# Earlier projections of the odd half sequences and another place for GpSimd's bias sums in an attention and expert block

## What is computed

```python
mod = (silu(c) @ wmod).reshape(B, 6, 1, 256)          # sa, ca, ga, sb, cb, gb
h = layernorm(x) * (1 + ca) + sa
qkv = h @ W_qkv.T + b_qkv                              # 16 heads
attn = softmax(Q @ K.T / 4 + causal)
x = x + ga * ((attn @ V) @ W_o.T + b_o)
h = layernorm(x) * (1 + cb) + sb
x = x + gb * experts(h)                                # top 2 of 8, w1 256x512, silu, w2 512x256
```

## Time and profile before

| | us |
|---|---|
| median of 3 runs | 1002.97 |
| lowest, highest | 1001.2, 1007.18 |
| the profiled execution | 1007.08 |
| its span, first to last instruction | 1005.0 |

### The profile page before, as it was taken

The page is one execution under the profiler, slowest core; times in us unless marked ns, Lnnn a source line. Parts: engine busy times, 40 slices in busy tenths (PEclk is TensorE's granted clock), DMA queues, the critical chain, the costliest instruction groups (busy, mean ns, idle before and its releaser), DMA issues.

```text
span 1005.0 us, 19371 instructions
## 1 busy us (share of the span) xinstructions
PE 894.9 (89%) x6100; PEld 532.1 (53%) x6174; DVE 724.2 (72%) x2323; ACT 582.1 (58%) x1271; POOL 355.6 (35%) x311
## 2 busy tenths in 40 slices
PE   5788799998989999889999997879899999999990
PEld 3443335333444443453543452523698899999880
DVE  8788766879756789857688769799637584444488
ACT  3335475766486677676676857657535433343563
POOL 1422021233324113345013444014386465655530
PEclk7899899999999999999999999989999999999996
DMA  8446337236234366250653746205313323222699
GB/s 280 126 65 128 52 64 166 53 50 142 54 48 112 55 118 132 76 77 22 127 95 107 154 73 192 68 25 173 97 52 121 96 70 100 81 74 75 197 295 314
DMA packets 83235, 110.61 MB, mean 110 GB/s; under 512 B 15930, under 2 KB 56434, under 8 KB 83138
## 3 DMA queue, kind: packets, MB, share of 16 engines
q1 hardware_dynamic: 75506, 89.45, 38.7%
q0 software_dynamic: 6816, 18.62, 5.9%
q10 hardware_dynamic: 816, 1.32, 0.4%
HBM read 69.42 MB, written 35.41 MB: 104 GB/s over the span
## 4 chain that ended last, share of the span: by engine, by line
PE 63%; DVE 13%; ACT 10%; issue 6%; POOL 3%; DMA 3%; SPq 1%; another core or an unknown queue 0%; ACTq 0%; POOLq 0%; DVEq 0%
PE PO L1642 10%; PE PY L1519 10%; PE PH L1519 9%; PE PS L1622 8%; PE PM L1599 7%; ACT PR L1008 4%; PE PHT L1727 3%; PE PX L1654 2%; PE PX L1568 2%; DVE MXF L1321 2%; DVE JK L1318 2%; PE PS L1626 2%; ACT SF L991 2%; PE PX L1671 1%; PE PX L1577 1%
## 5 line engine op out<-in xcount | busy, mean ns | idle before, releaser
L1008 ACT ACTIVATE PR<-PS 128x512 f32<-128x512 f32 (+3 forms) x768 | 334.5, 497 | 149.7 <-PE PS L1626 113.0
L1318 DVE CUSTOM_DVE_ANT_0 JK<-PM,MK 128x128 bf16<-128x128 f32 (+3 forms) x512 | 239.5, 484 | 58.0 <-PE PM L1599 56.7
L1599 PE MATMUL PM<-QK 128*128 128x512 bf16 (+3 forms) x725 | 233.9, 330 | 25.5 <-DVE MXF L1321 14.7
L1622 PE MATMUL PS<-QK 128*128 128x512 bf16 (+3 forms) x737 | 236.6, 332 | 17.8 <-ACT PR L1008 12.7
L1321 DVE TENSOR_REDUCE MXF<-PM 128x1 f32<-128x512 f32 x256 | 175.2, 684 | 78.2 <-PE PM L1599 61.4
L1622 PEld LDWEIGHTS PS<-QK 128*128 128x128 bf16 x768 | 75.4, 99 | 177.6 <-ACT PR L1008 111.5
L1642 PE MATMUL PO<-PR,V 128*17 128x512 f32 (+3 forms) x1536 | 163.3, 498 | 0.1
L1599 PEld LDWEIGHTS PM<-QK 128*128 128x128 bf16 x768 | 75.7, 99 | 100.1 <-DVE MXF L1321 35.5
L1519 PE MATMUL PY<-W2S,HT 128*128 x852 | 119.7, 290 | 2.7 <-issue 1.8
L1626 PE MATMUL PS<-MT,identb 128*128 128x128 bf16 x512 | 112.3, 221 | 1.9 <-issue 1.0
L1519 PE MATMUL PH<-W1S,XT 128*128 x426 | 112.6, 400 | 0.8 <-DVE W2S L1473 0.8
(11 more groups left out here) (269 smaller groups left out, 1179.8 us busy)
## 6 DMA issues: line engine op xcount, KB each, us to landing
QK<-SD SPq DMA_DIRECT2D x180, 128.0 KB
SD<-SP SPq DMA_DIRECT2D x42, 256.0 KB, 2.9
OP<-OS SPq DMA_DIRECT2D x64, 64.0 KB
LP<-LR SPq DMA_DIRECT2D x64, 64.0 KB
W1S<-in_w SPq DMA_DIRECT2D x8, 512.0 KB, 6.1
X<-XA SPq DMA_DIRECT2D x3, 1024.0 KB, 8.2
H2D<-XA SPq DMA_DIRECT2D x3, 1024.0 KB, 4.9
YG<-YT SPq DMA_DIRECT2D x12, 256.0 KB
```

The source lines that it names most:

```text
L1008: eng.activation(PR[:, slot, i, c0:512], PS[m % 3][:, c0:512], ACT.Exp, scale=0.25).then_inc(S["exp"].sem, 1)
L1318: eng.tensor_tensor_reduce(JK[:, jk % 2, 0:w], PM[m % 3][:, 0:w], MK[:, 512 - w:512], 1.0, -3.0e38, ALU.add, ALU.max, MXA[:, mb, h, qt:qt ...
L1599: eng.matmul(PM[m % 3][:, 0:128 * (k1 - k0)], QK[:, r, h, 0, qt * 128:(qt + 1) * 128], QK[:, r, h, 1, k0 * 128:k1 * 128], start=True, stop ...
L1622: last = eng.matmul(PS[m % 3][:, c0:512], QK[:, r, h, 1, j * 128:(j + 1) * 128], QK[:, r, h, 0, 512 * f + c0:512 * f + 512], start=True, s ...
```

## The change

The bias sums get places of their own for each sequence: b = 0 from (3, 8) to (2, 18), b = 1 from (3, 16) to (4, 1), b = 2 from (6, 12) to (6, 18), b = 3 from (10, 12) to (10, 18), with 1.5 slots between in place of 2. The four projections of the odd half sequences go from slots 11, 13, 15, 17 to 5, 7, 9, 11 of the groups -1, 3, 7 and 11; "qk_hi" and "qk_lo" go with them, "sd" stays.

```diff
@@ -167,11 +167,11 @@
         if b > 1:
             place(w - 1, 4, stats(b))
         for tp in range(4):
-            place(max(3, w + 1), (8, 16, 12, 12)[b] + 2 * tp, one("bias", b, tp))
+            place((2, 4, 6, 10)[b], (18, 1, 18, 18)[b] + 1.5 * tp, one("bias", b, tp))
     for u in range(2 * B):
         for n in range(4 if u else 0):
             which, half = n // 2, n % 2
-            place(2 * u - 3, (9, 11)[u % 2] + 2 * n, [(0, ("qk", u, which, half)), (1, ("qk_hi", u, which, half)), (2, ("qk_lo", u, which, half))])
+            place(2 * u - 3, (9, 5)[u % 2] + 2 * n, [(0, ("qk", u, which, half)), (1, ("qk_hi", u, which, half)), (2, ("qk_lo", u, which, half))])
```

## The result

The changed kernel takes 1015.21 us in the median (1012.51 to 1018.71), beside 1002.73 us for the kernel before in the same comparison (1001.2 to 1007.18). The ratio is 1.0116, with a 95% interval of 1.0088 to 1.0143. So the change costs about 12 us, where 1002.1 was forecast and 1006.5 was the upper end of the range. The profiled execution of the changed kernel took 1017.71 us, with a span of 1015.8; the mean granted clock is 0.968, as before.

A forecast was written before the change was run, and what follows sets the result against it. TensorE, busy for 89% of the span, was taken as the bound. Start -1.5, odd half sequences -0.9 and group 3's chain +1.5 gave -0.9 us, so 1002.97 became 1002.1 us, with a range of 997 to 1006.5.

The forecast's parts named there:

- Step (1): Start, projections of half sequence 1 moved ahead: net -1.5 us, between -3.4 and +1.0.
- +2.7: Start, stretch up to 71.76: two more projections of TensorE work add 2.7 us, between 1.7 and 3.4.
- -4.2: Start, stretch from 71.76 to 88.56: it loses two projections, casts, held chain steps and VectorE gaps, 4.2 us less.
- rival (A): The start grows, as the projections lie where TensorE has no room: +1.7 to +5.0 us, total 1005 to 1008; chance 0.13.
- Step (2): Projections of odd half sequences 3, 5, 7, moved within full groups: -0.3 us each, -0.9 together; bounds -0.5 and +0.5 each.
- the excess over a "v" group: An odd "qk" group costs 0.47 us more than a "v" group of equal TensorE work: all that can be gained.
- The test that I gave: Sign of a wrong forecast: scores wait over 1 us for ScalarE at slots 8 to 14 of odd groups.
- Step (3) and (5): Bias sums of b = 0, 2 and 3 in their new places: they cost nothing.
- Step (4): Bias sums of b = 1 meet the chain of group 3: chain 6.8 us, crow waits 2.2; +1.5 us, between 0 and +3.5.
- rival (B): Port rule in full at group 3's chain: 7.9 us and more, crow 3.5 us late, total 1004.1; chance 0.2.

The follow-up runs named there:

- e7: The kernel before with the cast and second subtraction (qk_lo) of every projection one slot sooner; 1001.04 us, ratio 0.9974.
- e6: The changed kernel with the cast and second subtraction (qk_lo) of every projection one slot sooner; 1006.7 us, ratio 1.0019.
- e8: The changed kernel with the odd half sequences' projections at slots 9, 11, 13, 15 in place of 5, 7, 9, 11; 1005.23 us, ratio 1.0004.
- e10: The changed kernel with the odd half sequences' projections at slots 9, 11, 13, 15 and qk_lo one slot sooner; 1000.94 us, ratio 0.9995.
- e1: The kernel before with only the bias sums in their new places, projections at their old slots; 1001.13 us, ratio 0.9991.
- e5: The changed kernel with the bias sums of b = 1 made to wait until the chain of group 3 is done; 1012.56 us, ratio 1.009 (two runs).
- e4: The kernel before with only the projections of half sequences 3, 5 and 7 moved to slots 5 to 11; 1011.39 us, ratio 1.0107 (five runs).

## Why the prediction was wrong

**Step (1), the start: -1.5 forecast, +2.7 measured.** The first stretch was to grow by the TensorE time of two projections, +2.7. The mark that has two projections ahead of it before and all four after is the third pv of group 0 (72.02 before, 76.75 after): from the first crow to it, 20.21 us became 25.16, +4.95 in place of +2.7. The two projections are 3.4 of that, and TensorE's waits for ScalarE, 1.39 us for the table and 0.30 at 76.05, are about the rest. From there to the first score of the second half (88.56 before, 91.98 after, 85 to 88 forecast) 16.54 us became 15.23, -1.3 where -4.2 was taken: two steps of the chain took 1.13 and 1.05 us, 1.8 us more than alone, where 0.9 was allowed for, TensorE waited 2.02 us for the maxima behind it, and the half clock took 1.1. Behind that 0.9 us comes back, where the kernel before has its own spell at half clock. So both terms failed: +2.7 counted TensorE alone and left out the table, and -4.2 counted VectorE's work and gaps and left out that TensorE waits while the chain is held, and that the clock may fall in this stretch.

The start of rival (A), +1.7 to +5.0, held the result, but partly by luck: its upper end let ScalarE's wait at the third and fourth copy, 1.65 us each from the earlier trace rows, stop the scores. The waits came (1.87 and 2.08 us), and cost the scores 0.30 us. The table load was in no case.

**Step (2), odd half sequences: -0.3 each forecast, +1.0 and +1.1 measured in groups 7 and 11.** With group 3's part, about +1.0, the three groups lost 3.2 us where -0.9 was forecast, an error as large as that of the start. The step said that TensorE's work is only moved inside a full group, and that the copies go on waiting as before. The wait at the third copy is indeed the same, 1.65 us (at the fourth 1.17 in place of 1.65). The step failed in taking an equal wait for an equal cost: 1.2 us of group 7 in the old place, 2.1 in the new one, by e7 and e6. That the exponentials behind the copy are of full width is not what makes the difference, as those behind the third copy of the kernel before and behind both in e8 are so too. What differs in the traces is how much work TensorE has beside it: slots 12 to 14 and 14 to 16 last 4.27 and 4.43 us in e8 with the wait and 4.26 and 4.43 without it (e10), so nothing waits there, while slots 10 to 12 and 12 to 14 of the changed kernel last 4.61 and 3.77 us with it and 3.74 and 2.59 without (e6). Where TensorE gets through two slots in 2.6 to 3.7 us, the next scores catch up with ScalarE and wait for its exponentials; that this is the reason is argued from these rows alone. Up to slot 18 the group lost 2.0 us (25.09 to 27.11) and got 1.0 back behind it. The row that would have said so was in front of me, as the earlier trace rows is a wait of an engine in whose order the exponentials stand. The bounds of 0.5 on either side came from the excess over a "v" group (0.47 us), that is from what is to be had, and this says nothing on what can be lost. That was the error of method. The test that I gave, a wait of the scores for ScalarE of over 1 us at slots 8 to 14, comes out at 0.70 + 0.26 + 0.56 us in group 7.

**Step (3) and (5), sums of sequences 0, 2, 3: 0 forecast.** Right: e1 is at 0.9991 with the odd groups unchanged.

**Step (4), the chain of group 3: +1.5 (0 to 3.5) forecast, 3.8 measured by e5.** The mechanism was right, and the step sizes too: four steps held by 0.6 to 1.0 us, the chain 6.26 us long (6.8 forecast), sums at 226 to 232. The term was mis-sized, since only the wait at crow was counted, 2.2 us less what comes back. Crow waits just 0.49 us. The rest lies ahead of it and behind it: VectorE's reductions stand in one order with the chain, TensorE's maxima wait 0.52 and 1.12 us for them, and slots 18 to 20 last 3.96 in place of 2.59 us. Before that the copies had cost the group its part of (2).

The Trainium skill, page "SBUF — State Buffer", section "Who interferes with whom", has the rule that a VectorE instruction with two SBUF inputs contends with a GpSimd instruction that reads SBUF. The runs agree: the same three steps take 0.89, 1.21, 0.81 us beside the sums and 0.17, 0.18, 0.17 us without. In full, as rival (B) had it, the rule gave +3.5, the nearest of my numbers for this step; but (B) put it all on crow, which waited 0.49 us, so the number is near by another path.

**The sum.** Of the 11.7 us between the forecast -0.9 and the measured +10.8, 4.2 are (1), 4.1 are (2) and 2.3 are (4); groups 12 and 13 (+2.2, in no case and not shown to be of the change), group 4 (-1.7) and the rest make up the difference. Every step was put beside TensorE's share of 89%, and the order of the others was left out. (A) ended at 1005 to 1008 because it took (2) and (4) from the forecast. The range failed by 9 us for two reasons: (2)'s bound on the side of a loss, and rivals that each let only one term go wrong, while (1) and (2) hang on the same order of GpSimd's subtractions.

## What to carry to other kernels

Before a step is moved, look at every engine that issues a part of it: where its part waits, what stands behind it there, and how much work the engine that needs this has meanwhile. A wait of 1.65 us cost a group 0.1 us at slots 13 and 15 and 2.1 at slots 9 and 11, by what is queued behind it and by how soon that is needed. What a place can gain bounds nothing on the other side; take for the loss the wait itself times the times that it occurs, and let all terms that hang on one wait go wrong together. And where a wait is for an engine's order and not for its work, as here GpSimd's two subtractions, mend the order first: one number did more (0.9974 alone, 0.9951 with the new places of the sums) than either placing of the projections. And when a mended kernel is to show that the causes are all found, give the mending to the kernel before as well, and compare these two.

## What the runs showed of the hardware

- The load of ScalarE's table takes 1.28 us, and stands ahead of the first exponential in its order: with idle time before it, it costs nothing; with a copy ahead of it, 1.39 us of TensorE. The exponential starts 0.01 us behind its end. The Trainium skill, page "ScalarE: Activation LUTs", section "What ACT_TABLE_LOAD costs", gives 1.28 us for the load and a drain of about 1.38 us more; no row here shows the latter.
- A cast from fp32 to bf16 in SBUF (L1294, 128 x 512) takes 0.42 us alone and 0.79 or 1.39 us beside GpSimd's subtractions in the changed kernel: it is held as the steps with two inputs are.
- The granted clock fell to its lower level (1.2 GHz, 0.61 in the mean of the stretch) in the changed kernel's start, after a stretch in which TensorE had waited for the table, the exponentials and the maxima, and stayed at 1.00 in the one trace in which only the wait for the table was gone, though the longest of these waits, 2.02 us just ahead of the fall, was still there. With the same start steps it fell to 0.50 at 88.16 us in the kernel before and at 86.32 in e1, and not at all near there in e4: whether it falls there differs between executions with the same steps.
